# Adding the experts' outputs in DRAM by accumulating scatters instead of writing two choices per token and adding them later

## What is computed

```python
x = x + conv0(ln(x))                     # layer 0: gated products with protein and compound pairs
t = x.reshape(B, 16384, 128)
t = t + mixture(ln(t))                   # 8 experts, the best two of each token
x = t.reshape(x.shape)
x = x + conv1(ln(x))                     # layer 1: as layer 0, with other weights
x = x + cell(ln(x))                      # a recurrent cell over 64 steps
# mixture: probs = softmax(t @ Wr + br); the two best experts of a token, weights that sum to 1
# y_e = gelu(xn @ W1[e] + b1[e]) @ W2[e] + b2[e];  out = w_first * y_first + w_second * y_second
```

## Time and profile before

| | us |
|---|---|
| median of 3 runs (2242.32 to 2259.24) | 2255.53 |
| the profiled execution | 2254.67 |
| its span, first to last instruction | 2252.9 |

### The profile page before, as it was taken

How to read it: one execution, slowest core, us unless ns; L and a number is a source line. 1 busy time by engine, 2 the same in 40 slices (tenths; PEclk the granted TensorE clock), 3 DMA queues, 4 the chain that set the end, 5 groups by cost and what they waited for, 6 DMA issues and landing times. The chain is left out here.

```text
span 2252.9 us, 48349 instructions
## 1 busy us (share of the span) xinstructions
PE 1768.2 (78%) x11055; PEld 1519.2 (67%) x11055; DVE 1463.0 (65%) x6046; ACT 1255.6 (56%) x3198; POOL 1185.7 (53%) x1844
## 2 busy tenths in 40 slices
PE   6967798896655540899999998477866579999995
PEld 5956688884443340799999998345864357878884
DVE  6965899966876651344444443798238977777776
ACT  5765999953443320556656655344446656655554
POOL 5865777740577777355555555788546520002220
PEclk9989999985555555899999999688986879999998
DMA  4021444422222144322222221773752100000004
GB/s 155 0 76 50 126 121 122 122 62 67 67 81 81 53 137 91 83 75 74 75 78 75 76 77 36 228 224 112 147 123 61 51 1 0 0 0 0 0 0 150
DMA packets 247581, 177.99 MB, mean 79 GB/s; under 512 B 93415, under 2 KB 213541, under 8 KB 247468
## 3 DMA queue, kind: packets, MB, share of 16 engines
q1 hardware_dynamic: 230060, 142.71, 23.6%
q0 software_dynamic: 17408, 34.00, 4.6%
HBM read 123.76 MB, written 54.97 MB: 79 GB/s over the span
## 5 line engine op out<-in xcount | busy, mean ns | idle before, releaser
L1597 POOL DMA_INDIRECT choices<-y,small x288 | 286.1, 993 | 220.5 <-ACT y L1627 150.2
L1279 POOL DMA_INDIRECT sorted_tokens<-work x256 | 249.6, 975 | 138.2 <-issue 77.5
L1660 PEld LDWEIGHTS banks<-w,hidden 128*128 128x128 f32 x2304 | 268.1, 192 | 5.5
L1660 PE MATMUL banks<-w,hidden 128*128 128x128 f32 x2304 | 268.5, 275 | 0.0
L1710 PEld LDWEIGHTS banks<-small 128*128 128x128 f32 x1536 | 193.2, 191 | 62.1 <-issue 32.2
L1710 PE MATMUL banks<-small 128*128 128x128 f32 x1536 | 225.3, 283 | 11.8 <-ACT small L1744 8.6
L1791 POOL COPY work_again<-small 128x128 f32 x128 | 38.3, 299 | 349.5 <-DVE small L1774 349.5
L388 PE MATMUL banks<-ident,small 128*128 128x128 f32 x640 | 119.6, 305 | 121.7 <-ACT small L375 77.4
L1701 PE MATMUL banks<-ab_tiles,small 128*128 (+1 forms) x768 | 210.2, 384 | 1.0 <-DVE small L1974 1.0
L1627 ACT ACTIVATE y<-y,small 128x128 f32<-128x128 f32 x288 | 92.3, 391 | 196.3 <-DVE y L1568 196.3
L375 ACT ACTIVATE small<-small 128x128 f32<-128x128 f32 x384 | 161.7, 483 | 32.4 <-POOL small L352 31.2
(11 more groups left out here) (267 smaller groups left out, 4562.7 us busy)
## 6 DMA issues: line engine op xcount, KB each, us to landing
small<-L_conv_protein_pair SPq DMA_DIRECT2D x128, 256.0 KB
rows<-sorted_tokens SPq DMA_DIRECT2D x72, 262.0 KB, 2.8
ab_tiles<-choices SPq DMA_DIRECT2D x32, 512.0 KB, 3.9
work_again<-L_conv_protein_pair SPq DMA_DIRECT2D x32, 512.0 KB, 7.5
x_tiles<-x SPq DMA_DIRECT2D x32, 256.0 KB, 3.7
work<-x SPq DMA_DIRECT2D x32, 256.0 KB, 2.8
after_mixture<-x_tiles SPq DMA_DIRECT2D x32, 256.0 KB, 2.2
work_again<-after_mixture SPq DMA_DIRECT2D x32, 256.0 KB, 2.7
```

The lines of the kernel that those rows point to most:

```text
L1279: pool.indirect_dma_start(out=self.sorted, out_offset=bass.IndirectOffsetOnAxis(ap=where[:, u // BATCH, u % BATCH * G + t, k:k + 1], axis= ...
L1597: pool.indirect_dma_start(out=self.out, out_offset=bass.IndirectOffsetOnAxis(ap=where[:, u, t:t + 1], axis=0), in_=y[:, u % 4, t, :], in_o ...
L1660: last = pe.matmul(out[:, t * P:(t + 1) * P], hidden[:, u % 2, h, t * P:(t + 1) * P], w2[:, u % 2, h * P:(h + 1) * P], start=h == 0 and t ...
```

## The change

The rows of `after_mixture` (the tokens, and 512 unused rows behind them) become the target of the experts' scatters. Dispatch stores the tokens there as soon as they are added (`keep_rows`). The experts' scatters add to these rows in DRAM (`compute_op=ALU.add`), without bounds check; rows of padding go to the unused rows. As a token has two experts, two scatters may name one row; so a slot's scatters wait until those of the slot before have landed. The second projection loads the rows like the first one and adds and stores nothing; ACT normalises three of its four tiles.

```diff
 # project_tokens (layer 1: src = rows of after_mixture, ahead = the pair tensors)
-        norm = Norm(chip, carve, (EPS_LNC, EPS_LN), banks=(0, 1), depth=4, by_act=2, by_pool=True)
+        norm = Norm(chip, carve, (EPS_LNC, EPS_LN), banks=(0, 1), depth=4, by_act=2 if ahead is None else 3, by_pool=True)
...
                 def load(n, u):
-                    merged.free(sp, n)
-                    sp.dma_start(pair[:, u, :, :, :], choices[:, bass.ds(n * G, G), :, :]).then_inc(pair_in[u], 16)
-
-                def store(n, u):
-                    merged.ready(sp, n)
-                    sp.dma_start(keep_in[:, bass.ds(n * G, G), :], tiles(n)).then_inc(stored[u], 16)
+                    if not isinstance(n, int) or n >= 4:
+                        sp.wait_ge(x_in[u], 4 * n - 4 * u)
+                    sp.dma_start(tiles(n), src[:, bass.ds(n * G, G), :]).then_inc(x_in[u], 16)
...
-                engine_loop(sp, GROUPS, 4, [(load, 0), (fetch, 0), (store, 3)])
-                for u in range(4):
-                    sp.wait_ge(stored[u], 16 * GROUPS // 4)
+                engine_loop(sp, GROUPS, 4, [(load, 0), (fetch, 0)], peel=4)
...
                 def stats(n, u):
-                    if src is not None:
-                        await_tiles(dve, x_in, n, u)
-                    else:
-                        summed.ready(dve, n)
-                        merged.done(dve.tensor_tensor(tiles(n), tiles(n), pair[:, u, :, 0, :], ALU.add))
-                        merged.ready(dve, n)
-                        dve.sem_inc(norm.paced, 1)
+                    await_tiles(dve, x_in, n, u)
                     norm.stats(dve, tiles(n), n, u)
...
                 def edge_mask(n, u):
-                    if choices is not None:
-                        await_tiles(pool, stored, n, u)
-                        pool.sem_inc(norm.paced, 1)
                     squashed.ready(pool, n * 2 + 1)
...
-                def add_choices(n, u):
-                    await_tiles(pool, pair_in, n, u)
-                    pool.sem_inc(norm.paced, 1)
-                    summed.done(pool.tensor_tensor(pair[:, u, :, 0, :], pair[:, u, :, 0, :], pair[:, u, :, 1, :], ALU.add))
 # Mixture.combine_and_dispatch, SP
-                    for ic in range(ICS):
-                        with sp.Fori(0, GROUPS // ICS // RING) as i:
-                            for u in range(RING):
-                                n = i * RING + (u + ic * (GROUPS // ICS))
-                                added.free(sp, n)
-                                sp.dma_start(before[:, u, :, :], src[:, ic, bass.ds((i * RING + u) * G, G), :]
-                                             ).then_inc(before_in[u], 16)
+                    rows = self.out[0:NP_ * NC_, :].rearrange("(p t) e -> p t e", p=P)
+
+                    def keep_rows(n):
+                        sp.dma_start(rows[:, n * G:(n + 1) * G, :], group(n)).then_inc(kept, 16)
+
+                    for n in range(GROUPS):
+                        ic, j = n // (GROUPS // ICS), n % (GROUPS // ICS)
+                        added.free(sp, n)
+                        sp.dma_start(before[:, n % RING, :, :], src[:, ic, j * G:(j + 1) * G, :]
+                                     ).then_inc(before_in[n % RING], 16)
+                        if n >= RING:
+                            keep_rows(n - RING)
                     norm.turned.ready(sp, GROUPS - 1)
+                    for n in range(GROUPS - RING, GROUPS):
+                        added.ready(sp, n)
+                        keep_rows(n)
...
                     sp.wait_ge(settled, 1)
+                    sp.wait_ge(emptied, 1)
...
                     sp.wait_ge(padded, 16 * EXPERTS)
+                    sp.wait_ge(kept, 16 * GROUPS)
 # POOL and DVE
-                    iota(copy_no, [[2, T]], 0, 2 * T)
+                    iota(copy_no, [[1, T]], 0, T)
+                    iota(unused, [[P, G]], NP_ * NC_, 1)
...
-                    dve.memset(empty[:, :, COPY:COPY + 1], NOWHERE).then_inc(emptied, 1)
                     dve.wait_ge(made, 2)
+                    dve.tensor_copy(empty[:, :, COPY], unused).then_inc(emptied, 1)
 # Mixture.experts, claim (DVE) and send (POOL)
-                        dve.scalar_tensor_tensor(where[:, u, :], rows[:, u, :, FIRST], lane, rows[:, u, :, COPY],
-                                                 ALU.not_equal, ALU.add)
+                        dve.tensor_scalar(where[:, u, :], rows[:, u, :, COPY], 1.0, None, ALU.mult)
...
                     def send(s, u):
+                        k = (u - 1) % 4
+                        if not isinstance(s, int) or s > 0:
+                            pool.wait_ge(sent[k], (s - (1 + k)) * (G * 16 // 4) + G * 16)
                         mixed.ready(pool, s)
                         pool.sem_inc(paced_pool, 1)
                         for t in range(G):
                             pool.indirect_dma_start(
                                 out=self.out,
                                 out_offset=bass.IndirectOffsetOnAxis(ap=where[:, u, t:t + 1], axis=0),
-                                in_=y[:, u % 4, t, :], in_offset=None, bounds_check=2 * NP_ * NC_ - 1,
-                                oob_is_err=False).then_inc(sent[u % 4], 16)
-                    engine_loop(pool, SLOTS, 8, [(send, 0)])
+                                in_=y[:, u % 4, t, :], in_offset=None, compute_op=ALU.add).then_inc(sent[u % 4], 16)
+                    engine_loop(pool, SLOTS, 8, [(send, 0)], peel=8)
```

More of the change, by code:

```diff
@@ L425, in raw_compound, with project_tokens @@
     return chip.spare()[:, NC_ * C:].rearrange("p (j c) -> p j c", j=NC_)
-def project_tokens(nc, chip, tag, par, src, choices=None, keep_in=None, ahead=None):
+def project_tokens(nc, chip, tag, par, src, ahead=None):
     gates, lins, (edge, edge_b) = par["gates"], par["lins"], par["edge"]
@@ L433, in project_tokens @@
     NS = NG + E
-    carve = Carve(chip.work if choices is None else chip.work[:, 0:P * C])
+    carve = Carve(chip.work if ahead is None else chip.work[:, 0:P * C])
     xf = chip.x
@@ L444, in project_tokens @@
         mask_in = chip.sem("mask_in")
-        if choices is not None:
-            pair = Carve(chip.spare()[:, 0:NC_ * C])(4, G, 2, E)
+        if ahead is not None:
             cp_in, chunk_in = chip.sem("cp_in"), chip.sem("chunk_in")
[L448 to L451, removed]
         x_in = [chip.sem(f"x_in{k}") for k in range(4)]
@@ L478, in _ @@
                 lin.load(sp)
-                if src is not None:
+                if ahead is None:
                     load_tiles(sp, xf, src, x_in)
@@ L508, in _ @@
                 gated.open(dve)
-                if choices is not None:
-                    merged.open(dve)
                 lin.fold(dve)
@@ L532, in gate @@
                         last = dve.scalar_tensor_tensor(
-                            chip.ab[:, bass.ds(tile, 1), 0:NL // C, :].rearrange("p a b c -> p (a b c)") if choices is None
+                            chip.ab[:, bass.ds(tile, 1), 0:NL // C, :].rearrange("p a b c -> p (a b c)") if ahead is None
                             else chip.planes()[:, :, bass.ds(tile, 1)].rearrange("p c t -> p (c t)"),
@@ L553, in edge_mask @@
                         mask[:, bass.ds(n * G, G)].unsqueeze(2).to_broadcast([P, G, E]), ALU.mult))
-                def add_choices(n, u):
-                    await_tiles(pool, pair_in, n, u)
-                    pool.sem_inc(norm.paced, 1)
-                    summed.done(pool.tensor_tensor(pair[:, u, :, 0, :], pair[:, u, :, 0, :], pair[:, u, :, 1, :], ALU.add))
-                stages = [(lambda n, u: norm.rstd(pool, n, u), 1), (edge_mask, 4)]
-                engine_loop(pool, GROUPS, 4, stages if choices is None else [(add_choices, 0)] + stages)
+                engine_loop(pool, GROUPS, 4, [(lambda n, u: norm.rstd(pool, n, u), 1), (edge_mask, 4)])
             @block.scalar
@@ L599, in _ @@
                 engine_loop(pe, GROUPS, 4, [(lambda n, u: norm.turn(pe, n, u), 0), (project, 1)])
-    return None if choices is None else (cp_in, chunk_in)
+    return None if ahead is None else (cp_in, chunk_in)
 class PairStream:
@@ L1107 @@
 SHARE, COPY, FIRST = range(E, ROW)
-NOWHERE = float(1 << 20)
 AHEAD = 8
@@ L1139, with __init__ @@
 class Mixture:
-    def __init__(self, nc, chip, p):
-        self.nc, self.chip, self.p = nc, chip, p
+    def __init__(self, nc, chip, p, rows):
+        self.nc, self.chip, self.p, self.out = nc, chip, p, rows
         self.sorted = nc.dram_tensor("sorted_tokens", (EXPERTS * REGION, ROW), F32).ap()
-        self.out = nc.dram_tensor("choices", (NP_ * NC_ * 2, E), F32).ap()
         ab = Carve(chip.ab[:, :, :, :].rearrange("p t s c -> p (t s c)"))
@@ L1192, in combine_and_dispatch @@
             paced, paced_act, paced_pool = (chip.sem(f"paced_{k}") for k in ("vector", "scalar", "gpsimd"))
-            empty, emptied, padded = work(G, ROW), chip.sem("emptied"), chip.sem("padded")
```

(10 more changed lines are left out.)

## The result

The changed kernel takes 2437.61 us (median of 4 runs, 2427.44 to 2446.64), beside it the kernel before 2251.52: a ratio of 1.0826 (95% interval 1.0786 to 1.0866). It is slower, as forecast, but the time lies above the range (2216 to 2390). The profiled execution took 2439.98 us, with a span of 2438.3, 185.4 more than before.

| stretch | before | after | difference |
|---|---|---|---|
| start to mask load (dispatch, experts) | 1414.7 | 1641.2 | +226.5 |
| mask load to last mask product | 151.0 | 110.3 | -40.7 |
| from there to the end | 687.2 | 686.8 | -0.4 |

What follows compares the result with a forecast made beforehand. PE was taken to bound the experts, POOL dispatch, POOL and DVE close together the second projection. 2254.7 us plus 75 lost in the experts minus 32 gained in the projection made 2298 us, range 2216 to 2390.

Steps and rivals of the forecast that it cites:

- The sum of a slot: Experts: 3 x 1.30 + 0.04 + 3.0 + 0.85 = 7.79 us a slot against 6.74, 75 us lost.
- three pitches: Experts, POOL: three times a scatter's duration plus the 0.30 us after it, forecast as 3 x 1.30 us.
- release to issue: Experts, POOL: time from the awaited landing to the next send's start, taken as 0.85 us.
- plain price: Experts, rival: adding costs next to nothing beside a plain scatter; slot 7.02 us, total 2243, no change; chance 0.26.
- I take 1.00, near the only rows there are: Experts: an adding scatter's duration on POOL, taken as 1.00 us between bounds of 0.96 and 1.92.
- Dear on POOL: Experts, rival: adding scatter lasts 1.45 us, slot 9.14, total 2393; chance 0.15, shared with a landing near 4 us.
- Hidden: Experts, rival: the wait fits POOL's idle 1.88 us, slot stays 6.74, total 2223, faster; chance 0.16.
- The landing: Experts: an adding scatter's time from issue to landing, taken as 3.0 us between 2.3 and 4.1.
- Dispatch at 0: Dispatch: 32 more stores of 256 KB on SP cost nothing; at most 39 us if the cover went.
- The clock: Experts: PE's clock may fall somewhat at 87% busy, but counts only below 0.87; within the range.
- The projection: Second projection: 32 us gained, the difference from the first projection's 118.7 us; at least 19, at most 43.
- some 3.1 us: Second projection: time per group after the change, 2.6 us each on POOL, DVE and ACT plus gaps; 4.10 before.

Runs made afterwards that it cites:

- the first experiment: The changed kernel with plain, overwriting scatters instead of adding ones, the wait for the slot before kept: 2228.58 us, ratio 0.9905 to the kernel before.

## Why the direction was right and the size wrong

*The sum of a slot* was built rightly: three pitches, the fourth's landing, and the way from release to issue. At the plain price it says 7.02 us and the first experiment measures 6.99. The step that failed is the duration of an adding scatter on POOL, "I take 1.00, near the only rows there are". It is 1.55, or 1.575 in the mean, and it enters three times. In the slot shown above:

| term | predicted | measured | difference |
|---|---|---|---|
| to the start of the fourth send | 3.94 | 5.65 | 1.71 |
| landing | 3.0 | 3.3 | 0.30 |
| release to issue | 0.85 | 0.96 | 0.11 |
| slot | 7.79 | 9.91 | 2.12 |

Four fifths of the miss are the duration. The last line is what is left of this slot; by the 35 slots with a traced landing it is 0.86, as forecast. Over the stage 71 x (9.855 - 7.79) = 147 us; less 8.7 that the projection gave more and with 4 of smaller ends, that is the 142 us between 2298 and the profiled execution's 2439.98.

*The argument behind that step.* I held against a dear scatter that the bounds check changes 0.958 us to 0.983 only. That speaks of work per row, and the runs show most of the price to be one per instruction, 0.47 us at 32 rows as at 64: the row I leaned on could not see it. The bounds that I set (0.96 to 1.92 us for the duration, 2.3 to 4.1 for the landing, 7.02 to 11.65 for the slot) hold all three measured values. What was too narrow was the choice between them: where the trace has no row for the operation itself, the nearest row of another operation was given most of the weight.

*The rivals.* "Dear on POOL" (1.45 us, a slot of 9.14, 2393 us) is what happened, dearer by 0.7 us a slot. I had given it 0.15, together with a late landing, and put the range's end just below it. "Hidden" falls: POOL is released by the DMA 65 times, and 0.86 us, in the median, are paid after a landing. "The plain price" falls with the duration; the first experiment shows what it would have been worth, a ratio of 0.9905. By the Trainium skill ("DMA: Bandwidth & Descriptors", Anatomy of one DMA) doubled bytes cost next to nothing and a slot would take 7.2 us, an estimate. For the plain scatter the trace is close to it (2.2 us of landing against 2.15); for the adding one it is not: the landing is 3.3 us, at 64 rows still 3.0, and POOL's own 0.59 us more isn't in that sum. The measurement decides. That the wait is needed, as the Trainium skill says on that page ("DMA: Bandwidth & Descriptors", Rules for kernel authors), no run here tests.

*The landing* was forecast from the plain 2.3 us and a load's 1.8, and 3.0 taken; 3.3 was measured, inside the bounds of 2.3 and 4.1. How much of the rise is the read of DRAM and how much the 144 packets, the runs don't separate: 64 rows with their half of the bytes land 0.3 us earlier.

*Dispatch at 0* was right: 326.9 us against 326.4 with the stores beside the sends, at a DMA share of 0.37 instead of 0.31.

*The clock* was rightly left out of the sum: the granted clock fell from 1.00 to 0.94 in the experts, but PE is busy 80% of that stretch and waits 92.9 us for rows, while POOL, which sets the pace, is released by a landing in 65 of the 71 slots after the first.

*The projection* gave 40.7 us, not 32, inside the bounds of 19 and 43. The step "some 3.1 us" a group was near (2.95); what was low is taking the difference from the first projection, whose product is wider and which has two tiles on ACT. That POOL is what the stage was bound by, and not DVE, which is busy a little longer in the earlier trace rows, is shown by the runs on the kernel before: with a fifth of DVE's busy time gone the stage did not get shorter, and with half of POOL's adds gone it did. The 0.81 us that I took from the earlier trace rows for a tile on DVE is the mean of two groups, 0.32 and 1.29, the long ones beside POOL's operations. So DVE gets more back than its share of the work: it is busy 2.43 us a group in the change, not 2.6.

## What to carry to other kernels

Before work is moved into the DMA, ask what the issuing engine pays for each instruction, and whether the order that an addition needs puts that price, the landing and the release in series: two costs that are small alone (18 and 51 us here) made 216 to 221 together, because each alone had been partly under another engine's time. Where the trace has no row for the operation that a change introduces, do not take its nearest relative for the likeliest value: here the plain scatter gave the price's lower bound and no more. A mean duration can hide two groups; look at the timeline before you call it the cost of the work. And when an edit leaves out data, look whether a later loop runs as often as before, and compare by stages.

## What was not expected of the hardware

- An indirect scatter that adds in DRAM holds POOL for 1.55 us against 0.96 for a plain one of the same 128 rows of 512 bytes; 0.47 of the 0.59 us between them is there at 32 rows already, and half rows save nothing.
- It makes 144 packets instead of 32. By the queue's share (11.0% of 16 x 2438.3 us, less 256 plain scatters at 0.19 us an engine, which is 4.6% of before's span over 544 scatters) each DMA engine is occupied some 0.76 us by one adding scatter: four times the plain one, though less than POOL's 1.85 us for each. Without the wait the adding scatters start every 1.85 us, so the DMA engines don't set the pace.
- It lands 3.3 us after its start instead of 2.2 (first experiment, same rows).
- After a landing POOL takes 0.86 us in the change and 0.88 in the first experiment (medians) until the next scatter starts, while between sends that follow each other at once there are 0.30. Each wait on a landing pays that difference once.
- Some of the small operations on POOL (line 346, otherwise 0.23 us) and of DVE's normalised tiles (otherwise 0.32 us) take 0.58 and 1.29 us, and each long one lasts until 0.08 to 0.09 us after a large operation of the other engine that it overlaps: 28 of 28 on POOL in the kernel with three tiles on ACT, 32 of 32 on DVE in the kernel before.
